# A transformer layer's kernel: the stage in front of the attention loop as one token order per engine, maxima and magnitude sums taken off GpSimd, loads in another order, a shorter guard

## The reference, cut to what matters

```python
def bitnet_linear(x, weight, scale_param):
    s = jnp.maximum(jnp.mean(jnp.abs(weight), axis=1), 1e-08)
    binary_w = jnp.sign(weight / s[:, None])
    y = jnp.einsum('bsi,oi->bso', x, binary_w)
    y = y * (s * scale_param)[None, None, :]
    return jnp.nan_to_num(y, nan=0.0, posinf=1000000.0, neginf=-1000000.0)

xn = _layernorm(x, axis=-1)                      # x: (1, 1024, 512)
q, k, v = (bitnet_linear(xn, w, scale) for ...)  # 32 query heads, 8 key heads, head size 16
attn = softmax(q k^T / 4); o = bitnet_linear(attn v, o_weight, o_scale)
hidden = silu(xn @ gate_w.T) * (xn @ up_w.T)     # gate_w = gate_t (-1, 0, 1) * gate_s[:, None], 1792 rows
out = x + o + hidden @ down_w.T
```

## Time and profile before

| | |
|---|---|
| time, median of 3 runs (lowest, highest) | 536.28 us (535.72, 536.89) |
| the profiled execution: its own time | 537.09 us |
| its span, first to last instruction | 535.3 us |
| mean granted TensorE clock | 0.988 |
| busy share of the span | PE 92%, DVE 81%, ACT 66%, POOL 19% |
| chain that ended last | PE 74%, DVE 12%, ACT 7%, DMA 3%, issue 3% |

### The profile page before, as it was taken

How to read it: one execution, slowest core, us unless ns; L and a number is a source line. 1 busy time by engine, 2 the same in 40 slices (tenths; PEclk the granted TensorE clock), 3 DMA queues, 4 the chain that set the end, 5 groups by cost and what they waited for, 6 DMA issues and landing times.

```text
span 535.3 us, 9756 instructions
## 1 busy us (share of the span) xinstructions
PE 493.0 (92%) x3889; PEld 163.0 (30%) x3889; DVE 434.6 (81%) x502; ACT 351.1 (66%) x636; POOL 104.3 (19%) x144
## 2 busy tenths in 40 slices
PE   0598996889999999999999999999999998999995
PEld 0355442333334222222222222222222222223442
DVE  5939939977677899999999999999999952223797
ACT  1553333422322999999999999999999985774000
POOL 4603315334342300000000000000000112241021
PEclk9999999889999999999999999999999998999999
DMA  7711454431210370211021202101120213362221
GB/s 236 201 41 44 122 120 85 112 79 23 37 22 1 45 132 24 59 39 59 22 59 38 58 24 59 39 28 53 39 59 22 63 34 106 79 171 64 82 78 59
DMA packets 29956, 36.37 MB, mean 68 GB/s; under 512 B 6544, under 2 KB 20752, under 8 KB 29912
## 3 DMA queue, kind: packets, MB, share of 16 engines
q1 hardware_dynamic: 20600, 24.19, 15.4%
q0 software_dynamic: 8304, 10.95, 10.7%
q10 hardware_dynamic: 1008, 0.61, 0.5%
HBM read 30.62 MB, written 10.35 MB: 77 GB/s over the span
## 4 chain that ended last, share of the span: by engine, by line
PE 74%; DVE 12%; ACT 7%; DMA 3%; issue 3%; SPq 0%; POOL 0%; ACTq 0%; DVEq 0%
PE ps L1174 22%; PE ps L1055 16%; PE ps L1139 13%; PE ps L1107 9%; PE ps L1064 8%; ACT room L664 5%; DVE nmx L804 3%; PE ps L1200 3%; PE ps L1036 3%; DVE room L741 1%; DMA hlo<-x 1%; DMA ga<-r_scratch 1%; ACT osb L675 1%; DVE y L800 1%; DVE gr L794 1%
## 5 line engine op out<-in xcount | busy, mean ns | idle before, releaser
L804 DVE TENSOR_REDUCE nmx<-ps 128x1 f32<-128x1024 f32 x256 | 292.9, 1213 | 2.6 <-PE ps L1064 2.4
L664 ACT ACTIVATE room<-ps 128x512 f32<-128x512 f32 x512 | 274.2, 597 | 23.0 <-PE ps L1139 12.9
L1174 PE MATMUL ps<-room,vcur 128*32 128x256 f32 (+1 forms) x1912 | 160.0, 406 | 4.4 <-ACT osb L675 4.2
L1139 PE MATMUL ps<-qst,kB 50*128 50x512 f16 x512 | 150.1, 384 | 2.4 <-ACT room L664 1.7
L1064 PE MATMUL ps<-kA,qst 48*128 48x512 f16 x512 | 145.5, 382 | 1.7 <-DVE nmx L804 1.7
L1055 PE MATMUL ps<-room,wf 128*128 128x512 f16 x448 | 106.5, 394 | 7.5 <-DVE room L890 7.4
L1174 PEld LDWEIGHTS ps<-room,vcur 128*32 128x32 f32 x1912 | 37.7, 108 | 100.2 <-issue 53.0
L1139 PEld LDWEIGHTS ps<-qst,kB 50*128 50x128 f16 x512 | 30.9, 93 | 114.6 <-ACT room L664 101.2
L1055 PEld LDWEIGHTS ps<-room,wf 128*128 128x128 f16 x448 | 43.6, 101 | 67.8 <-issue 23.6
L645 ACT ACTIVATE room<-ps,gsc 128x512 f32<-128x512 f32 x28 | 19.2, 686 | 66.7 <-PE ps L1055 66.7
L505 POOL TENSOR_TENSOR shp<-mxs,ones 16x128 f16<-16x128 f32 x16 | 7.2, 448 | 226.9 <-ACT mxs L600 226.9
(11 more groups left out here) (127 smaller groups left out, 299.8 us busy)
## 6 DMA issues: line engine op xcount, KB each, us to landing
qst<-q_scratch SPq DMA_DIRECT2D x32, 192.0 KB, 3.4
o_scratch<-osb SPq DMA_DIRECT2D x16, 256.0 KB, 2.3
q_scratch<-parts SPq DMA_DIRECT2D x12, 256.0 KB
hlo<-x SPq DMA_DIRECT2D x8, 256.0 KB, 7.0
parts<-x POOLq DMA_DIRECT2D x8, 256.0 KB, 3.4
wf<-gate POOLq DMA_DIRECT2D x14, 128.0 KB, 3.0
wf<-up POOLq DMA_DIRECT2D x14, 128.0 KB, 3.1
wd<-down POOLq DMA_DIRECT2D x1, 1792.0 KB, 13.5
```

The costliest lines, as they stand in the source:

```text
L664: nc.scalar.activation(probs[:, s % 2, r, :], ps[:, score_bank(entry(j, i)), :], ACT.Exp, scale=gam_reg[par][r]).then_inc(scores_free, 1)
L804: nc.vector.tensor_reduce(nmx[:, hf, idx:idx + 1], bank_pair(idx % 2), AX.X, ALU.max, negate=True).then_inc(rows_free, 1)
L1139: nc.tensor.matmul(ps[:, score_bank(e), :], kB[low:low + SROWS, par, kt % (TT // 2) * P:(kt % (TT // 2) + 1) * P], qst[low:low + SROWS, pa ...
L1174: mm = nc.tensor.matmul(ps[32 * r:32 * r + 32, 7, of], vcur[:, par, key_tile(r, j), :], probs[:, s % 2, r, of], start=(j == 0 and part == ...
```

## The change

- **Orders.** The plain code in front is gone: the strings now begin with tokens for it. On DVE M is the statistics of a tile, H and R the two pieces of the inverse deviation, N normalising, L the remainder, J the factor of the hidden layer; on PE X is the transposes of a tile, K the spreading of the gain, G0/U0 and G1/U1 the gate and up halves of F0 and F1; on ACT D is the deviation, B the absolute values and N the signs of wk, wq and wv (each now by itself), C the copy of a tile, Y the absolute values of wo. The steps behind are in another order too.
- **Maxima.** The largest |gate_s * up_s| is found by a transpose on PE (K0), a reduction of one row on DVE (J1), and a matmul of K=1 with ones (K1). The largest |v| is not measured any more: a bound of it, H times the largest scale of v, comes from `svb` by four small DVE operations (V0); the output's scale takes it in step S1.
- **Magnitudes.** For q, k and v POOL adds nothing; PE accumulates over the four chunks, 20 products of one column and 4 of 128 columns in place of 5 and 1. The sum for wo stays on POOL, but in place in `wot` and behind F10 (`WO_AT`); S1 moves from behind F2 to behind A7.
- **Loads.** gate and up scales first on ACT's queue; sob and dsb on SP's; the weights of F0 behind the last tile of x, those of F1 to F3 and wo behind wv.
- **Guard.** Four operations for five; it also serves the tail.

```diff
-    pe_order = ("F0 S0 P0 Z0 P1 Z1 P2 Z2 P3 F1 F2 S1 F3 P4 F4 P5 F5 F6 F7 F8 F9 A0 F10 A1 F11 A2 A3 F12 "
+    pe_order = ("K0 X0 X1 X2 X3 K1 S0 X4 X5 G0 X6 Z0 X7 U0 P0 Z1 P1 Z2 G1 P2 U1 F2 F3 P3 F4 P4 F5 P5 F6 F7 A0 F8 F9 "
...
+    dve_order = ("M0 M1 J0 M2 M3 H0 M4 R0 N0 J1 N1 M5 N2 N3 M6 M7 H1 L0 R1 L1 N4 N5 L2 L3 S0 Z0 N6 N7 J2 L4 V0 L5 L6 "
...
+    act_order = ("D0 B0 C0 B1 B2 D1 C1 C2 N2 C3 C4 C5 W0 C6 N0 C7 F0 N1 E0 E1 X0 F1 F2 X1 Y0 F3 E3 F4 V2 E4 F5 X3 F6 "
...
             load_weights(wv, NH * D + KV, wv_loaded)
+            sp.wait_ge(wv_loaded, 16)
             sp.dma_start(wot[:, :, :], wo.rearrange("(c p) o -> p c o", p=P)).then_inc(wo_loaded, 16)
+            sp.dma_start(sob[:, :], so.to_broadcast([P, H])).then_inc(sob_loaded, 16)
+            sp.dma_start(dsb[:, :], sd.to_broadcast([P, H])).then_inc(dsb_loaded, 16)
...
             nc.gpsimd.memset(ones[:, :], 1.0).then_inc(consts_ready, 1)
-            load_ffn(0)
...
             pool.wait_ge(x_loaded[TT - 1], 16)
+            load_ffn(0)
+            pool.wait_ge(wv_loaded, 16)
             for f in range(1, WF_BUFS):
                 load_ffn(f)
-            magnitudes(mags, 0)
-            pool.wait_ge(gain_ready, 1)
-            nc.gpsimd.partition_all_reduce(gain[:, 1:2], gain[:, 0:1], P, RMAX).then_inc(gmax_ready, 1)
+
+            def magnitudes():
+
+                pool.wait_ge(abs_wo_ready, 1)
+                nc.gpsimd.tensor_tensor(wot[:, 0:2, :], wot[:, 0:2, :], wot[:, 2:4, :], ALU.add).then_inc(mag_step, 1)
+                pool.wait_ge(mag_step, 1)
+                nc.gpsimd.tensor_tensor(wot[:, 0, :], wot[:, 0, :], wot[:, 1, :], ALU.add).then_inc(mag_ready, 1)
...
-                if w == V_AT:
-                    pool.wait_ge(vmax_ready, 1)
-                    nc.gpsimd.partition_all_reduce(vg[:, 1:2], vg[:, 0:1], P, RMAX).then_inc(vred_ready, 1)
...
                 hidden_low(w)
+                if w == WO_AT:
+                    magnitudes()
...
+                elif kind == "B":
+                    loaded, c0, nc_ = weights[n]
+                    act.wait_ge(loaded, 16)
+                    nc.scalar.activation(absolute[:, :, c0:c0 + nc_], wt[:, :, c0:c0 + nc_], ACT.Abs).then_inc(abs_ready, 1)
...
                 mask, repl, less = gb[:, 0:n_], ga[:, 0:n_], gr[:, 0:n_]
-                nc.vector.tensor_scalar(repl, v_, 0.0, HUGE, ALU.is_gt, ALU.mult).then_inc(guard_step, 1)
-                nc.vector.tensor_scalar(less, v_, 0.0, HUGE, ALU.is_lt, ALU.mult).then_inc(guard_step, 1)
+                nc.vector.tensor_scalar(less, v_, HUGE, -HUGE, ALU.min, ALU.max).then_inc(guard_step, 1)
                 nc.vector.tensor_scalar(mask, v_, 0.0, 0.0, ALU.mult, ALU.not_equal).then_inc(guard_step, 1)
-                dve.wait_ge(guard_step, guards + 2)
-                nc.vector.tensor_tensor(repl, repl, less, ALU.subtract).then_inc(guard_step, 1)
+                dve.wait_ge(guard_step, guards + 1)
+                nc.vector.scalar_tensor_tensor(out=repl, in0=v_, scalar=0.0, in1=less, op0=ALU.max,
+                                               op1=ALU.min).then_inc(guard_step, 1)
...
-                    if PROJ[n] == V_:
-                        dve.wait_ge(guarded, 2 * n + 2)
-                        nc.vector.tensor_reduce(vg[:, 0:1], y[:, n % 2, :], AX.X, ALU.max,
-                                                apply_absolute_value=True).then_inc(vmax_ready, 1)
...
                 if part == 0:
+                    pe.wait_ge(abs_ready, 3)
                     pe.wait_ge(consts_ready, 2)
                     for col in range(QT + 1):
-                        nc.tensor.matmul(ps[:, 7, col:col + 1], mags[:, col * P:(col + 1) * P], ones[:, 0:1],
-                                         start=True, stop=True)
+                        for c in range(HC):
+                            nc.tensor.matmul(ps[:, 7, col:col + 1], absolute[:, c, col * P:(col + 1) * P], ones[:, 0:1],
+                                             start=(c == 0), stop=(c == HC - 1))
```

More of the change, by code:

```diff
@@ L74, in layer_kernel @@
     T_AT = [n for kind, n in pe_order[:pe_order.index(("T", 0))] if kind == "F"][-1]
+    NORM_GROUPS = [(0, 4), (4, 8)]
+    SIGNS = [n for kind, n in act_order if kind == "N"]
+    SUM_AT = [n for kind, n in pe_order[pe_order.index(("S", 1)):] if kind == "A"][0]
+    WO_AT = 10
     assert T_AT % 2 == 0 and len(PROJ) == 6
     assert pe_order.index(("T", 0)) > pe_order.index(("A", UNITS - 1))
+    assert [n for kind, n in pe_order if kind in "FU"] == list(range(FU))
+    assert dve_order.index(("A", SUM_AT - 1)) < dve_order.index(("S", 1)) < dve_order.index(("A", SUM_AT))
+    assert [n for kind, n in dve_order if kind == "F"] == list(range(FU))
     for order in (pe_order, dve_order):
-        assert [n for kind, n in order if kind == "F"] == list(range(FU))
         assert [n for kind, n in order if kind == "A"] == list(range(2 * UNITS))
@@ L81, in layer_kernel @@
     VY = PROJ.index(V_) % 2
-    V_AT = [n for kind, n in dve_order[:dve_order.index(("V", PROJ.index(V_)))] if kind == "F"][-2]
     WF_BUFS = 4
@@ L199, in layer_kernel @@
         absolute = qst[:, :, :, :, :].rearrange("p a b h n -> p (a b h n)").bitcast(F32)[:, 0:HC * NQKV]
-        mags = absolute[:, 0:NQKV]
+        absolute = absolute.rearrange("p (c n) -> p c n", c=HC)
         kA = sb("kA", [P, 2, HALF], F16)
@@ L567, in xhi_copy @@
                                ps[:, i % 4, :].rearrange("p (c n) -> p c n", c=HC)).then_inc(xhi_ready, 1)
[L569 to L588 removed]
+            weights = [(wk_loaded, NH * D, KV), (wq_loaded, 0, NH * D), (wv_loaded, NH * D + KV, KV)]
             def hidden_high(n):
@@ L603, in _ @@
             for kind, n in act_order:
-                if kind == "E" and PROJ[n] != V_:
+                if kind == "D":
+                    of = slice(*NORM_GROUPS[n])
+                    act.wait_ge(stats_ready, NORM_GROUPS[n][1])
+                    nc.scalar.activation(std[:, of], mv[:, of, 1], ACT.Sqrt, bias=eps[:, 0:1]).then_inc(std_ready, 1)
+                    if n == 0:
+                        act.dma_start(svb[:, :], sv.to_broadcast([P, KV])).then_inc(vec_loaded, 16)
+                elif kind == "C":
+                    xhi_copy(n)
+                elif kind == "B":
+                    loaded, c0, nc_ = weights[n]
+                    act.wait_ge(loaded, 16)
+                    nc.scalar.activation(absolute[:, :, c0:c0 + nc_], wt[:, :, c0:c0 + nc_], ACT.Abs).then_inc(abs_ready, 1)
+                elif kind == "N":
+                    loaded, c0, nc_ = weights[n]
+                    act.wait_ge(loaded, 16)
+                    nc.scalar.activation(sgn[:, :, c0:c0 + nc_], wt[:, :, c0:c0 + nc_], ACT.Sign).then_inc(sign_ready, 1)
+                elif kind == "E" and PROJ[n] != V_:
                     col = QT if PROJ[n] == K_ else PROJ[n]
@@ L617, in _ @@
                     act.wait_ge(wo_loaded, 16)
[L618 to L621 removed]
+                    nc.scalar.activation(sgno[:, :, :], wot, ACT.Sign).then_inc(sign_wo_ready, 1)
+                elif kind == "Y":
+                    act.wait_ge(sign_wo_ready, 1)
+                    nc.scalar.activation(wot, wot, ACT.Abs).then_inc(abs_wo_ready, 1)
                 elif kind == "V":
                     act.wait_ge(vscale_ready, 1)
+                    act.wait_ge(guarded, 2 * n + 2)
                     act.wait_ge(consts_ready, 3)
@@ L808, in _ @@
             for kind, n in dve_order:
-                if kind == "E" and PROJ[n] == V_:
+                if kind == "M":
+                    x_stats(n)
+                elif kind == "H":
+                    half_variance(n)
+                elif kind == "R":
+                    inverse_std(n)
+                elif kind == "N":
+                    normalize(n)
+                elif kind == "L":
+                    x_low(n)
+                elif kind == "J":
+                    hidden_factors(n)
+                elif kind == "E" and PROJ[n] == V_:
                     dve.wait_ge(proj_ready, n + 1)
@@ L975, in _, with transpose_x @@
             pe.wait_ge(consts_ready, 1)
-            for i in range(TT):
+            def transpose_x(i):
                 pe.wait_ge(xn_ready, i + 1)
@@ L1017, in project @@
                 what = PROJ[n]
-                pe.wait_ge(sign_ready, 1 if n == 0 else 2)
+                pe.wait_ge(sign_ready, SIGNS.index({K_: 0, V_: 2}.get(what, 1)) + 1)
                 pe.wait_ge(xlo_ready, TT)
```

187 lines of the change are left out of this document (85 added, 102 removed), and 6 rows, old and new, of the table dve_order.

## The result

| | before | changed |
|---|---|---|
| median of the runs (lowest, highest) | 536.0 us (535.29, 536.89) | 521.47 us (519.96, 521.79) |
| the profiled execution: own time, span | 537.09, 535.3 | 519.96, 518.2 |
| start of P0, the first projection | 34.0 | 34.2 |
| first scores | 176.14 | 160.59 |
| from the first scores to the end | 359.16 | 357.61 |

What follows compares the result with a forecast made beforehand. PE's work in a row bounds the front: S0 at 17.0 + 141.3 + 1.0 gives first scores at 159.3, 16.8 earlier; with 0.3 for the last guard, 17.1 us off, 519.2 us. Range 516.5 to 525.5; the forecast's own 516.5 to 521 got 0.64.

Steps and rivals of the forecast that it cites:

- What bounds: Ahead of the first scores: PE's work in a row from 26.08 us, with 10.6 us of waits for DVE and slow-clock matmuls.
- D: Rival, 0.03: waits for DVE only move to the next place with their slow clock; 10.6 + 3.4 us return, 533.2 us.
- Cover by DVE: From first guard to last split, DVE has 49 us of work against PE's 61, so 12 us of slack.
- Start of S0: At the front: S0 starts at 17.0 us, when ACT has the absolute values of wq and wv; bounds 16.3 and 18.7.
- A: Rival, 0.16: loads decide; late gate and up scales, or wq and wv, delay S0 to 18.7 or 19.6; 521 to 523.
- S0's growth: In S0 on PE: 15 more one-column products and 3 more wide ones add 3.0 + 1.0 = 4.0 us.
- Slow clock behind S0: At F0's dense matmuls: 1.0 us lost to the slow clock, the middle of bounds 0 and 2.0.
- The late transposes: X4, X5 and X6 now come behind S0 on PE: 3 x 1.12 = 3.4 us more; X7 was already counted.
- Sum: S0's start 17.0 plus PE's work 141.3 plus 1.0 of slow clock: first scores at 159.3 us, 16.8 earlier.
- The rest of the program: From the first scores to the end: code, order and waits kept, so moved and not changed, but for the last guard's 0.3 us.
- B: Rival, 0.14: DVE still bounds in front of the scores; half the waits and slow F remain, 7 us; about 526.
- C: Rival, 0.03: PE's clock stays at 1.2 GHz behind S0, each F or P costing 3.4 us more; up to 553.

Runs made afterwards that it cites:

- the kernel with spare products: Changed kernel plus eight spare 32-bit products of 512 columns on PE ahead of S0, their results unread: 520.81 us, ratio 0.972 to the kernel before.

## Why the prediction was right

- **What bounds, and D.** PE's work in a row was the bound, and the waits and the slow F behind them were really gone: no wait for DVE behind S0 until the scores, no F at a slow pace behind P0. Waits moved nowhere. This was the largest term, 10.6 + 3.4 us, and it came in whole. But the cover that the prediction worked out for it was DVE's relief, and with the guard and the bound alone 4.1 us of waits and a slow F of 3.0 stayed. These 7 us went with the rest of the change, most likely with its order. The signs fit too: the longest idle time of POOL from its first remainder to the first scores was 5.6 us, and two row maxima and an F came every 4.1 us.
- **Cover by DVE: right.** Even with the old guard no wait appeared.
- **Start of S0: right, 16.2 for 17.0.** wq landed at 13.72 (14.6 forecast), and ACT took 2.44 as expected. A was not the case: the two scales, first in their queue now, landed in 1.8 and 2.6 us, where the earlier trace rows has 7.7.
- **S0's growth: mis-sized.** "15 x 0.20 = 3.0 more" and "3 x 0.33 = 1.0 more" took the duration from a row at full clock. Here 20 products took 8.7 us, 0.43 each, and 4 wide ones 1.9: 10.6 us where 5.3 were counted. The prediction placed a slow clock only behind S0, as at most 2.0 us for the dense matmuls; S0 itself ran at the pace of 1.2 GHz from its first product to its last.
- **Slow clock behind S0: 0.5 for 1.0.** The first half of F0 took 2.26 us against 1.73 of the second. The Trainium skill, page TensorE: Matmul & The Clock Gate, Part 1, would have the slow time used up by S0. The trace does not bear that out: after 10.6 us of S0 without a gap the first matmuls of F0 were still slow, and in the kernel with spare products the clock fell in the midst of S0. The 0.5 us is also one draw: in the four profiles with S0 and all in front of it unchanged but for the loads this half of F0 took 2.47 to 3.05 us in the timelines, 0.6 to 1.2 over its 1.89 at full pace, so 1.0 was a fair price.
- **The late transposes: too dear.** X4 to X7 were charged at 1.12 us each, 4.5 in all. They took 1.71 + 0.44 + 0.49 = 2.6, because the 1.12 is a tile's time behind idle time; by the pace of the others, 0.44 to 0.49 at the upper level and 0.85 behind S0, it was a slow one.
- **Sum.** PE's work from S0 on was 144.4 us for 142.3: 5.3 too little for S0, 1.8 too much for the transposes, 0.5 for the clock, and 0.9 that no row places and that I count to the old kernel's net work. With the start 0.8 early that is 160.6 for 159.3. The two errors of 5.3 and 1.8 + 0.5 + 0.8 + 0.9 offset each other; the total is better than its terms.
- **The rest of the program: moved, not changed**, as expected, and 0.3 for the guard is lost in its spread. That the profiled execution came out at exactly the 17.1 us forecast is luck: the one of before had a slow stretch behind 447 us, and this one had none. The medians differ by 14.5, and 521.5 is 2.3 us over the forecast of 519.2.
- **B and C** did not happen. POOL's sum for wo did stretch DVE's operation beside it, 2.18 us for 1.27 usually, and POOL's next remainder took 2.13 for 1.15, but that did not reach PE:

```profile
97.98 2.18 DVE L882 SCALAR_TENSOR_TENSOR parts<-y,q_up,parts 128x1024 f16<-128x1024 f32 x1
```

## What to carry to other kernels

Take the duration of a moved instruction from a row with the same state of PE's clock, not only of the same shape: products at the very front cost twice their price. If PE is to add up by products with one column, look at what fills them. Here it was the loading of weights, and making the numbers 16 bits wide took 9.5 us out of S0 and 7.2 off the first scores. And with waits, take away the work and the order apart: less work on DVE and POOL cured one kind (products); the other (row maxima) went only with the whole change, which also had another order. And before two profiled executions are compared, look in both for stretches at the lower clock: one of them was 1.5 of the 17.1 us here.
